# Bias loads issued from ScalarE behind the last probabilities, and the rows' factor ahead of SyncE's larger loads

## The chip, the cores and the metric

The kernel runs on one core of a Trainium2 chip. The metric is the device time of one execution in microseconds (us), lower is better; the figure of a kernel is the median of its runs. TensorE (PE) multiplies matrices, VectorE (DVE), ScalarE (ACT) and GpSimd (POOL) do elementwise work, and SyncE (SP) only issues DMAs here. ACT and POOL can issue DMAs as well. A profile says "SPq" or "ACTq" for work of an engine's sequencer, such as the issue of a DMA.

## What is computed

One block on 128 sequences of 128 tokens with 256 features, in float32: cross attention with 16 heads and a bias on the scores, and then a mixture of 8 experts of which each token uses one.

```python
x = x + tanh(g_xattn) * attn(layernorm(x), ctx, ctx, bias)   # bias: 128 x 16 x 128 x 128
x = x + tanh(g_ffn) * moe(layernorm(x))

# attn: q, k, v projections (low-rank parts added), D = 16
scores = einsum('bqhd,bkhd->bhqk', q * D ** -0.5, k) + bias
out = einsum('bhqk,bkhd->bqhd', softmax(scores), v)
# moe: idx = argmax(softmax(x @ Wg + bg)); out = (gelu(x @ W1[idx] + b1[idx])) @ W2[idx] + b2[idx]
```

The bias is by far the largest input: 128 x 16 x 128 x 128 numbers, which is 1 MB for each sequence.

## The kernel before

The attention goes through the sequences in order. Every engine has a `step(i, k)` of its own; step k of all engines together works on several sequences at different lags. `seq(i, k, lag)` is the sequence k - lag, so a negative lag means work ahead of time. There are 128 such steps and some more at either end; behind them comes the expert phase, from about 1700 us on. The queries and keys are projected for two sequences at a time, so steps come in pairs: even steps do more than odd ones.

**The rows' factor.** The layer norm of the queries is applied late: PE projects the raw x, and DVE multiplies the result by 1/sigma of each row (`scale_queries`, line 1104, which reads the tile `RS`). That factor is needed along the free dimension on all partitions, while it is computed one number to a partition. So it goes through device memory: for sequence k + 4, SP stores 128 numbers of 4 bytes each from `ln` (a part of `x2n`) to `rs_dram` (`send_scale`, line 357), waits until that store has landed (`rs_out`, line 365), and loads the row of 128 numbers back, broadcast to all partitions, into `RS` (`spread_scale`, line 367, 64 KB). The store waits for POOL's power (`rs_ok`, lines 507 and 509), which waits for DVE's statistics at the end of the step before.

**SyncE's queue.** All hardware-issued loads of the attention stand on SP's one queue, in the order of `step`: the factor's store, on even steps the context `CT` for two sequences (256 KB, line 380), `x_sb` (128 KB, line 385), on even steps `XT`, the turned x for the queries (256 KB, line 390), then the wait for the store and the load of `RS`, then the bias of sequence k + 3 into `sc` in two halves of 512 KB (line 403). The bias of k + 3 may be written once PE has turned all of sequence k - 1 (`tr_ready`), whose slot of four it takes.

**The other engines.** In step k DVE adds the bias to the scores (line 1039), takes the maxima (1045), then, once PE has turned the output (`o_ready`), the statistics of x of sequence k + 5 (1055, which needs `x_sb`), the residual (1152), on even steps `scale_queries` (1104), and the second statistics (1060, 1068). POOL subtracts the maxima (485), makes the norm factors (507, 509, 514), adds a bias to x (522), and scatters the rows of sequence k - 9 to `rows_dram` (540). A row buffer of eight is written again one step after its scatter is issued, so line 507 also waits for that scatter's landing (`x2_out`). ACT computes the probabilities of sequence k - 1 in four parts (`probs`, line 887), and each is behind PE's turning of that part.

Of the kernel before, what the change touches and what calls it, by code (L numbers as in the profile page):

```python
# [12 lines left out]
P = 128  # L13
# [3 lines left out]
HEADS = 16  # L17
# [6 lines left out]
U = 8  # L24
# [72 lines left out]
def flamingo_block(nc, x, x_turned, ctx_in, bias, wqT, wkT, wvT, bv, lora_in,  # L97
                   w1, w2, b2, consts, out):
    ctx = ExitStack()
    with ctx:  # L100
        def sb(name, shape, dt=F32):
            return ctx.enter_context(nc.sbuf_tensor(name, shape, dt))

        def sem(name):
            return ctx.enter_context(nc.semaphore(name))
# [29 lines left out]
        sc = sb("sc", [P, 4, HEADS * P])  # L135
# [107 lines left out]
        s_w, s_ab = {w: sem(f"s_w{w}") for w in "qkv"}, sem("s_ab")  # L243
# [7 lines left out]
        bias_in = [sem(f"bias_in{i}") for i in range(4)]  # L251
# [8 lines left out]
        tr_ready, pt_ready = sem("tr_ready"), sem("pt_ready")  # L260
# [35 lines left out]
        def seq(i, k, lag):  # L296

            t = At(i, k - lag, U)
            if isinstance(i, int) and not 0 <= i * U + k - lag < N:
                return None  # L300
            return t
# [45 lines left out]
        def _(sp):  # L347
# [6 lines left out]
            def send_scale(t):  # L354
                sp.wait_ge(rs_ok, t.n(1, 1))
                sp.nop(nofuse=True)
                sp.dma_start(rs_dram[t.n()], ln[:, (t.k - 7) % 8, 0, 0:1]).then_inc(rs_out, 16)  # L357
# [10 lines left out]

            def step(i, k):
                behind = seq(i, k, -4)  # L370
                if behind and not (isinstance(i, int) and k < 0):
                    send_scale(behind)
                t = seq(i, k, -6) if k > FIRST else None
                if t and t.slot(2) == 0:
                    if t.reached(8):
                        sp.wait_ge(k_ready, t.per(2, KC, -3 * KC))
                        sp.nop(nofuse=True)
                        sp.wait_ge(v_ready, t.n(1, -6))
                        sp.nop(nofuse=True)
                    sp.dma_start(CT[:, t.k // 2 % 4], ctx_in[t.per(2)]).then_inc(ctx_inn[t.k // 2 % 4], 16)  # L380
                if t:
                    if t.reached(8):
                        sp.wait_ge(x2_ok, t.n(1, -7))
                        sp.nop(nofuse=True)
                    sp.dma_start(x_sb[:, t.slot(8), :], x_seq[t.n()]).then_inc(x_in[t.slot(8)], 16)
                if behind and behind.slot(2) == 0:
                    if behind.reached(4):
                        sp.wait_ge(q_ready, behind.per(2, KC, -KC))
                        sp.nop(nofuse=True)
                    sp.dma_start(XT[:, behind.k // 2 % 2], x_turned[behind.per(2)]).then_inc(xT_in[behind.k // 2 % 2], 16)  # L390
                if behind and isinstance(i, int) and k < 0:
                    send_scale(behind)
                if behind:
                    spread_scale(behind)
                t = seq(i, k, -3)
                if t:
                    if t.reached(4):
                        sp.wait_ge(tr_ready, t.n(4, -12))  # L398
                        sp.nop(nofuse=True)
                    if not t.reached(1):  # L400
                        sp.wait_ge(s_w["k"], 16)
                    for h in range(0, HEADS, 8):
                        sp.dma_start(sc[:, t.slot(4), h * P:(h + 8) * P],  # L403
                                     bias[t.n(), :, h * P:(h + 8) * P]).then_inc(bias_in[t.slot(4)], 16)
                if isinstance(i, int) and k == 2:
                    sp.wait_ge(vacant_ok, 3)
                    sp.dma_start(rows_dram[DUMMY:DUMMY + FT, :].rearrange("(p a) r -> p (a r)", p=P),
                                 vacant[:]).then_inc(vacant_out, 16)
                    sp.dma_start(b2_all[:].rearrange("p e h -> p (e h)"), b2.rearrange("(a e) h -> a (e h)", a=1)
                                 .partition_broadcast(P)).then_inc(b2_in, 16)  # L410
# [428 lines left out]
        def _(act):  # L839
            for n in range(3):  # L840
                act.dma_start(lora[STRIP * n:STRIP * n + RANK, :], lora_in[n]).then_inc(s_ab, 16)
            for w, wt in (("v", wvT), ("q", wqT), ("k", wkT)):
                act.dma_start(W[w][:], wt).then_inc(s_w[w], 16)
            act.wait_ge(s_id, 16)
            nc.scalar.activation(tg[:], g_raw, ACT.Tanh).then_inc(s_seta, 1)

# [36 lines left out]
            def probs(t, q):  # L883
                act.wait_ge(tr_ready, t.n(4, q + 1))
                if q == 0 and t.reached(2):
                    act.wait_ge(ot_ready, t.n(1, -1))
                nc.scalar.activation(PT[:, t.slot(2), 512 * q:512 * q + 512], turn_bank(t, q)[:],  # L887
                                     ACT.Exp).then_inc(pt_ready, 1)

            def step(i, k):  # L890
# [42 lines left out]
                if prev and not scored:  # L933
                    probs(prev, 2)
                    probs(prev, 3)
                if qry and qry.slot(2) == 0:
                    queries(qry)

# [468 lines left out]
```

## Time and profile before

| what | us |
|---|---|
| median of 3 runs | 2010.56 (2008.79 to 2016.85) |
| the profiled execution | 2008.24 |
| its span | 2006.4 |
| PE, DVE, ACT, POOL busy | 1373.5, 1137.6, 774.8, 1000.9 |
| expert phase | from about 1700 to the end |

The span is what the profile covers; the execution's own time is 1.8 us more. Busy time is summed over both phases. A wait is listed as the engine and line that waited, and what ended the wait. The chain is followed back from the last instruction to whatever released each step. A landing time of a DMA runs from its issue to its completion. In a table of stretches, "DMA share" is the share of the 16 DMA engines' time that packets took.

### The profile page before, as it was taken

How to read it: one execution, taken by the hardware profiler on the slowest of the kernel's cores; microseconds unless marked ns; L12 is line 12 of the kernel's file. 1: busy time of each engine (PE TensorE's matmuls, PEld its weight loads, DVE VectorE, ACT ScalarE, POOL GpSimd, SP SyncE). 2: the span in 40 equal slices, each digit the busy share in tenths (PEclk: the TensorE clock that was granted, in tenths of full speed). 3: DMA queues.
4: the chain of work that ended last, by engine and by line, in shares of the span. 5: the costliest groups of instructions: out<-in, count | busy, mean ns of one | idle time of the engine just before them, and what ended most of it. 6: DMA issues, size and time to landing. Idle time of an engine off the chain costs nothing.

```text
span 2006.4 us, 41833 instructions
## 1 busy us (share of the span) xinstructions
PE 1373.5 (68%) x12568; PEld 1150.0 (57%) x12568; DVE 1137.6 (57%) x2377; ACT 774.8 (39%) x1660; POOL 1000.9 (50%) x1051
## 2 busy tenths in 40 slices
PE   4656666666666566666666656666666666999998
PEld 3545555555555455555555545555555555788887
DVE  3445555565655555556555555555555555855655
ACT  1333334444434334444443334444333344533333
POOL 2334544555554455455554544555445454655455
PEclk7777878888877778888887888888777788999999
DMA  4555655555555555556555555556555554599896
GB/s 114 125 120 126 132 129 119 115 130 130 131 131 114 122 129 128 102 129 131 131 128 110 128 128 123 110 126 131 121 114 131 129 129 113 198 297 278 277 284 212
DMA packets 156729, 288.73 MB, mean 144 GB/s; under 512 B 36836, under 2 KB 72166, under 8 KB 156544
## 3 DMA queue, kind: packets, MB, share of 16 engines
q1 hardware_dynamic: 142992, 252.02, 54.7%
q0 software_dynamic: 12624, 34.62, 4.7%
q10 hardware_dynamic: 1056, 1.39, 0.2%
q8 instruction: 28, 0.46, 0.1%
q14 instruction: 29, 0.24, 0.1%
HBM read 251.89 MB, written 36.98 MB: 144 GB/s over the span
## 4 chain that ended last, share of the span: by engine, by line
DMA 71%; PE 14%; SPq 9%; issue 5%; POOL 0%; DVE 0%; ACT 0%; POOLq 0%; ACTq 0%
DMA rs_dram<-x2n 70%; PE two L789 5%; PE bank L803 5%; SPq L403 5%; SPq L367 2%; PE two L777 1%; DMA RS<-rs_dram 1%; SPq L357 0%; PE two L596 0%; PE bank L630 0%; PE bank L621 0%; DMA w_sb<-in_w 0%; PE two L646 0%; SPq L398 0%; DMA rows_dram<-vacant 0%
## 5 line engine op out<-in xcount | busy, mean ns | idle before, releaser
L596 PE MATMUL two<-KT,QT 32*128 32x256 f32 x2048 | 206.1, 532 | 599.6 <-DVE QT L1104 564.0
L485 POOL TENSOR_TENSOR sc<-sc,negmax 128x1024 f32<-128x1024 f32 x256 | 484.1, 1893 | 149.9 <-DVE negmax L1045 144.3
L596 PEld LDWEIGHTS two<-KT,QT 32*128 32x128 f32 x2048 | 125.1, 250 | 636.6 <-DVE QT L1104 493.4
L1039 DVE TENSOR_TENSOR sc<-two,sc 128x1024 f32<-128x1024 f32 x256 | 312.1, 1219 | 130.2 <-PE two L596 128.8
L507 POOL TENSOR_SCALAR ve<-mv 128x2 f32<-128x2 f32 (+1 forms) x135 | 30.5, 226 | 667.8 <-DVE mv L1068 654.9
L1045 DVE TENSOR_REDUCE negmax<-sc 128x8 f32<-128x1024 f32 x256 | 312.4, 1220 | 16.2
L621 PE MATMUL bank<-cst,sc 128*128 128x128 f32 x2032 | 287.6, 287 | 0.1
L887 ACT ACTIVATE PT<-bank 128x512 f32<-128x512 f32 x508 | 279.5, 603 | 15.6 <-PE bank L621 14.4
L853 ACT ACTIVATE QT<-QT,cst 128x256 f32<-128x256 f32 x128 | 58.0, 500 | 559.4 <-DVE QT L1104 559.4
L621 PEld LDWEIGHTS bank<-cst,sc 128*128 128x128 f32 x2032 | 239.1, 148 | 32.7 <-issue 32.2
L1055 DVE BATCH_NORM_STATS2 st<-x_sb 128x6 f32<-128x256 f32 x128 | 53.9, 421 | 358.0 <-DMA x_sb<-in_x 356.1
L630 PE MATMUL bank<-PT,V 128*32 128x128 f32 x4096 | 181.9, 334 | 0.3 <-ACT PT L887 0.3
L555 POOL DMA_INDIRECT out<-og,ids x120 | 118.4, 986 | 115.0 <-issue 106.8
L1104 DVE TENSOR_TENSOR QT<-two,RS 128x256 f32<-128x256 f32 x128 | 48.3, 419 | 218.2 <-DMA RS<-rs_dram 218.2
L630 PEld LDWEIGHTS bank<-PT,V 128*32 128x32 f32 x4096 | 141.6, 137 | 48.6 <-issue 25.7
L881 ACT COPY OT<-bank 128x512 f32<-128x512 f32 x128 | 75.0, 586 | 231.0 <-PE bank L630 226.9
L540 POOL DMA_INDIRECT rows_dram<-x2n,slot_i x128 | 135.1, 1056 | 29.5 <-issue 25.4
L646 PE MATMUL two<-CT,wk 128*128 128x256 f32 x512 | 126.7, 391 | 13.0 <-DVE QT L1104 13.0
L864 ACT ACTIVATE KT<-two,bk_half,cst 128x256 f32<-128x256 f32 x256 | 124.0, 563 | 29.1 <-PE two L646 28.7
L746 PE MATMUL bank<-wv,CT 128*128 128x256 f32 x512 | 133.0, 383 | 0.0
L646 PE MATMUL two<-XT,wq 128*128 128x256 f32 x512 | 126.0, 389 | 4.4 <-DVE sc L1039 3.5
L803 PE MATMUL bank<-CT,hT 128*128 128x256 f32 x516 | 122.6, 379 | 0.0
(159 smaller groups left out, 2059.0 us busy)
## 6 DMA issues: line engine op xcount, KB each, us to landing
sc<-in_bias SPq DMA_DIRECT2D x256, 512.0 KB
w_sb<-in_w SPq DMA_DIRECT2D x69, 257.0 KB, 3.7
CT<-in_w SPq DMA_DIRECT2D x69, 256.0 KB, 3.8
xg<-rows_dram SPq DMA_DIRECT2D x63, 272.0 KB, 3.8
x_sb<-in_x SPq DMA_DIRECT2D x128, 128.0 KB, 11.0
CT<-in_ctx_in SPq DMA_DIRECT2D x64, 256.0 KB
XT<-in_x_turned SPq DMA_DIRECT2D x64, 256.0 KB
RS<-rs_dram SPq DMA_DIRECT2D x128, 64.0 KB
```

Source lines behind the costliest of these rows:

```text
L485: nc.gpsimd.tensor_tensor(s, s, m, ALU.add).then_inc(sub_ok, 1)
L540: nc.gpsimd.indirect_dma_start(rows_dram, bass.IndirectOffsetOnAxis(ap=slot_i[:, g, j:j + 1], axis=0), x2n[:, t.slot(8), :], None).then_in ...
L596: ins = mm(b_s[j][:, 2 * P * c:2 * P * c + 2 * P], QT[rows, pair, c, P * sq:P * sq + P], KT[rows, pair, c, sq].rearrange("p e k -> p (e k) ...
L621: ins = nc.tensor.transpose(turn_bank(t, q)[:, P * h:P * h + P], sc[:, t.slot(4), o:o + P], ident)
L630: ins = mm(b_x[CELL * j:CELL * j + CELL, P * (h // 4):P * (h // 4) + P], V[:, t.slot(8), h, :], PT[:, t.slot(2), P * h:P * h + P], start=T ...
L646: ins = mm(b_s[o][:, 0:2 * P], W[w][:, c, o * P:o * P + P], moving[:, c, :], start=(c == 0), stop=(c == KC - 1))
L746: ins = mm(b_v, CT[:, pair, c, tok:tok + P], W["v"][:, c, :], start=(c == 0), stop=(c == KC - 1))
L803: ins = mm(y_half, hT[:, t.slot(2), c, a * P:a * P + P], w2_of(t)[:, c * HID:c * HID + HID], start=(c == 0), stop=(c == KC - 1))
L864: ins = nc.scalar.activation(KT[:, pair, o, :, e, :], b_s[o][:, 0:2 * P].rearrange("p (s k) -> p s k", s=2), ACT.Identity, bias=bk_half[:, ...
L887: nc.scalar.activation(PT[:, t.slot(2), 512 * q:512 * q + 512], turn_bank(t, q)[:], ACT.Exp).then_inc(pt_ready, 1)
L1039: nc.vector.tensor_tensor(s, two[h][:], s, ALU.add).then_inc(s_used, 2)
L1045: nc.vector.tensor_reduce(negmax[:, t.slot(2), 8 * h:8 * h + 8], sc[:, t.slot(4), 1024 * h:1024 * h + 1024].rearrange("p (h k) -> p h k", ...
```

## The change

The bias loads leave SP. ACT issues them, for the first three sequences right after the weights, and from then on for sequence k + 3 at the end of ACT's step k, behind the last two probabilities of sequence k - 1 and ahead of the queries' bias. ACT has by then waited for PE's last turn of k - 1, so no wait is issued for it. On SP the load of `RS` moves up, right behind its store: it is now ahead of `CT`, `x_sb` and `XT` instead of behind them. For the very first steps the old place of the store holds one step less than before (k < -1 instead of k < 0).

```diff
@@ SP, step
-                if behind and not (isinstance(i, int) and k < 0):
+                if behind and not (isinstance(i, int) and k < -1):
                     send_scale(behind)
+                    spread_scale(behind)
...
-                if behind and isinstance(i, int) and k < 0:
+                if behind and isinstance(i, int) and k < -1:
                     send_scale(behind)
-                if behind:
                     spread_scale(behind)
-                t = seq(i, k, -3)
-                if t:
-                    if t.reached(4):
-                        sp.wait_ge(tr_ready, t.n(4, -12))
-                        sp.nop(nofuse=True)
-                    if not t.reached(1):
-                        sp.wait_ge(s_w["k"], 16)
-                    for h in range(0, HEADS, 8):
-                        sp.dma_start(sc[:, t.slot(4), h * P:(h + 8) * P],
-                                     bias[t.n(), :, h * P:(h + 8) * P]).then_inc(bias_in[t.slot(4)], 16)
@@ ACT, ahead of the steps
+            def load_bias(t):
+                for h in range(0, HEADS, 8):
+                    act.dma_start(sc[:, t.slot(4), h * P:(h + 8) * P],
+                                  bias[t.n(), :, h * P:(h + 8) * P]).then_inc(bias_in[t.slot(4)], 16)
+
+            for n in range(3):
+                load_bias(At(0, n, U))
@@ ACT, step
                 if prev and not scored:
                     probs(prev, 2)
                     probs(prev, 3)
+                t = seq(i, k, -3)
+                if t and t.reached(3):
+                    load_bias(t)
                 if qry and qry.slot(2) == 0:
                     queries(qry)
```

On SP, an odd step inside the loop, before. ISA and REGISTER_ALU rows are waits and address arithmetic; `sc<-in_bias` is the bias.

```order
L357 ISA [waits rs_ok]
L357 DMA rs_dram<-x2n 128x1
L385 ISA [waits x2_ok]
L385 DMA x_sb<-in_x 128x256
L364 REGISTER_ALU [waits scaled_ok]
L367 DMA RS<-rs_dram 128x128 [waits rs_out]
L398 REGISTER_ALU
L403 ISA [waits tr_ready]
L403 DMA sc<-in_bias 128x1024
L403 ISA
L403 DMA sc<-in_bias 128x1024
```

The same queue in the changed kernel, an even step and the start of the next.

```order
L357 ISA [waits rs_ok]
L357 DMA rs_dram<-x2n 128x1
L364 REGISTER_ALU [waits scaled_ok]
L367 DMA RS<-rs_dram 128x128 [waits rs_out]
L381 ISA [waits k_ready,v_ready]
L381 DMA CT<-in_ctx_in 128x512
L384 REGISTER_ALU
L386 ISA [waits x2_ok]
L386 DMA x_sb<-in_x 128x256
L391 DMA XT<-in_x_turned 128x512 [waits q_ready]
L357 ISA [waits rs_ok]
L357 DMA rs_dram<-x2n 128x1
```

Before, the bias stood between the load of `RS` and the next store; now the context, x and the turned x stand there, and the bias is gone from the queue.

On ACT, the end of an even step in the loop, before.

```order
L874 ACTIVATE x2n<-x,x2n 128x256 [waits x2t_ready,shift_ok]
L925 COPY V<-bank 128x16x16 [waits ot_ready,v_ready]
L931 COPY x2T<-two 128x256 [waits lt_ready,x2t_ready]
L887 ACTIVATE PT<-bank 128x512 [waits tr_ready] x2
L853 ACTIVATE QT<-QT,cst 128x256 [waits scaled_ok]
L853 ACTIVATE QT<-QT,cst 128x256
```

The same place in the changed kernel.

```order
L872 ACTIVATE x2n<-x,x2n 128x256 [waits x2t_ready,shift_ok]
L923 COPY V<-bank 128x16x16 [waits ot_ready,v_ready]
L929 COPY x2T<-two 128x256 [waits lt_ready,x2t_ready]
L885 ACTIVATE PT<-bank 128x512 [waits tr_ready] x2
L837 DMA sc<-in_bias 128x1024 x2
L851 ACTIVATE QT<-QT,cst 128x256 [waits scaled_ok]
L851 ACTIVATE QT<-QT,cst 128x256
```

Two DMA issues have come in behind the last two probabilities and ahead of the queries; nothing else moved on ACT. PE, DVE and POOL run the same instructions in the same order as before.

## Rows read from the trace of the kernel before

**Rows 1.** The page: busy time of the engines, and the chain by line.
```profile
PE 1373.5 (68%) x12568; PEld 1150.0 (57%) x12568; DVE 1137.6 (57%) x2377; ACT 774.8 (39%) x1660; POOL 1000.9 (50%) x1051
...
DMA rs_dram<-x2n 70%; PE two L789 5%; PE bank L803 5%; SPq L403 5%; SPq L367 2%; PE two L777 1%; DMA RS<-rs_dram 1%; SPq L357 0%; PE two L596 0%; PE bank L630 0%; PE bank L621 0%; DMA w_sb<-in_w 0%; PE two L646 0%; SPq L398 0%; DMA rows_dra
```
**Rows 2.** Who waited for whom: us in total, times, longest.
```profile
PE two L596 <- DVE QT L1104: 564.0, 61, 12.4
...
DVE st L1055 <- DMA x_sb<-in_x: 356.1, 102, 7.6
...
DVE QT L1104 <- DMA RS<-rs_dram: 218.2, 64, 10.0
...
SPq L365 <- DMA rs_dram<-x2n: 1166.8, 126, 11.9
```
**Rows 3.** The chain in order of time: start, us, what; two steps.
```profile
1006.43 0.33 SPq L367
...
1008.66 10.21 DMA rs_dram<-x2n
1019.01 0.33 SPq L367
...
1020.77 12.20 DMA rs_dram<-x2n
1033.11 0.33 SPq L367
```
**Rows 4.** The load of RS: durations of its issue, first and last start.
```profile
L367 SPq DMA_DIRECT2D RS<-rs_dram x128: 327/333/336, 16.0 to 1698.3; - x128
```
**Rows 5.** Busy time by stretch: PE, PEld, DVE, ACT, POOL, PE clock, DMA share, GB/s.
```profile
1020.00:1023.00 3.00, 3.00 (x57) 2.28 (x56) 2.30 (x6) 1.53 (x5) 1.94 (x3) 1.00 0.20 16
1023.00:1028.00 5.00, 4.87 (x33) 4.27 (x31) 3.82 (x5) 3.10 (x8) 4.76 (x5) 1.00 0.73 267
1028.00:1033.00 5.00, 0.00 (x0) 0.00 (x0) 0.00 (x0) 0.56 (x2) 1.00 (x1) 0.90 0.00 0
...
1012.00:1013.00 1.00, 1.00 (x12) 0.85 (x16) 0.80 (x6) 0.83 (x2) 0.22 (x1) 0.50 1.07 412
```
**Rows 6.** Instructions in order of time: start, us, what, idle time before it.
```profile
1009.35 0.78 SPq L380 DMA_DIRECT2D CT<-in_ctx_in  x1
...
1011.10 0.33 SPq L390 DMA_DIRECT2D XT<-in_x_turned  x1
1011.13 0.76 DVE L1104 TENSOR_TENSOR QT<-two,RS 128x256 f32<-128x256 f32 x2 [3.36 <-DMA RS<-rs_dram]
...
1019.68 0.86 SPq L403 DMA_DIRECT2D sc<-in_bias  x2
```
**Rows 7.** Chain and stretches at the start, before any bias was loaded.
```profile
15.98 0.33 SPq L367
...
16.88 8.28 DMA rs_dram<-x2n
...
20.00:25.00 5.00, 0.00 (x0) 0.00 (x0) 0.61 (x2) 0.00 (x0) 1.51 (x3) 0.67 0.00 0
...
9.00:10.00 1.00, 1.00 (x3) 0.82 (x4) 0.00 (x0) 0.00 (x0) 0.00 (x0) 0.50 0.96 350
```
**Rows 8.** DVE in order of time, from one step's start to the next stall.
```profile
1014.16 1.22 DVE L1039 TENSOR_TENSOR sc<-two,sc 128x1024 f32<-128x1024 f32 x1 [1.05 <-PE two L596]
...
1021.87 1.22 DVE L1039 TENSOR_TENSOR sc<-two,sc 128x1024 f32<-128x1024 f32 x1 [0.46 <-PE two L596]
...
1026.74 0.25 DVE L1141 RECIPROCAL rden<-bank 128x16 f32<-128x16 f32 x1
```
**Rows 9.** Landing times: x of 1000 to 1100 us, and the scatter issued at 1024.15.
```profile
DMA to landing us min/median/max: 10.3/10.8/11.2
...
1021.82 0.22 POOL L507 TENSOR_SCALAR ve<-mv 128x2 f32<-128x2 f32 x1 [0.82 <-DMA rows_dram<-x2n,slot_i]
...
1024.15 1.06 POOL L540 DMA_INDIRECT rows_dram<-x2n,slot_i  x1 [0.18 <-issue]
...
DMA to landing us min/median/max: 9.9/9.9/9.9
```

## The prediction, made before the changed kernel was run

> **What bounds the kernel now.** I read the chain by line first. The store of the rows' factor to device memory holds 70% of the span, while no engine is busy for more than 68% of it [rows 1]. The list of waits says the same: SyncE waited for that store 126 times, 1166.8 us in all. The long waits of the others hang on the same queue: DVE for x (356.1 us) and for the spread factor (218.2 us), and PE for the queries which DVE scales with that factor (564.0 us) [rows 2].
>
> The chain in order of time shows a loop inside one queue [rows 3]. The load of RS is issued at 1019.01, the next store at 1020.77, it lands at 1032.97, and the next load of RS is issued at 1033.11. The step before took 1006.43 to 1019.01. So a step is 12.6 and 14.1 us there. Over the whole phase there are 128 loads of RS from 16.0 to 1698.3 [rows 4]: 127 steps of 13.25 us. This is the period to change; the 308 us behind it are the expert phase, which the change does not touch.
>
> What fills the 14.1 us is seen in the stretches [rows 5]. From 1020 to 1023 the DMA engines move 16 GB/s: 3.0 us x 16 is 48 KB, nearly all of the 64 KB of RS. From 1023 to 1028 they move 267 GB/s, 1.3 MB: the bias, x and the scatter. From 1028 to 1033 they move nothing, and only then does the store land. Its data is 512 bytes. So the store has a tail of some 5.4 us of its own behind the last byte ahead of it, and the bias stands ahead of it because it was issued first on the same queue. The bias itself takes about 3.7 us: 1 MB at some 285 GB/s, between the 267 of that stretch and the 412 of the best microsecond.
>
> Is the tail the store's own, or a result of the bias? The start of the trace answers it [rows 7]. There only RS (issued 15.98) and one x load are ahead of the store issued at 16.88; no bias has been loaded yet. From 20 to 25 us the engines move nothing, and the store lands at 25.16. The tail is again over 5 us, with nothing around it. I conclude that the change can take the bias out of the path, and not the tail.
>
> **The change, part by part.** *The bias leaves SyncE's queue.* Its 3.7 us ahead of each store go, and the issue of two DMAs, 0.86 us [rows 6], which lay on the path too.
>
> *RS moves ahead, and CT, x and XT now stand between RS and the next store.* Before, they were behind the store and moved in its tail. Now they are ahead of it. For an odd step (RS, x, store) the trace has this very order at the start: from the issue of RS at 15.98 to the store's landing at 25.16 are 9.18 us [rows 7]. With 0.14 us from landing to the next issue of RS (1032.97 to 1033.11 [rows 3]) that is 9.3 us. An even step has CT and XT besides, 512 KB: at 412 GB/s [rows 5] 1.3 us, so 10.6 us. Their issue does not matter more: from CT at 1009.35 to the end of XT at 1011.43 are 2.1 us [rows 6], less than RS and its start-up take (4.7 us from its issue at 1006.43 to DVE's use at 1011.13 [rows 3, 6]). Mean of the two: 10.0 us.
>
> *The bias moves beside it, from another queue.* It still uses the same DMA engines. The cost lies between nothing (it moves in the store's 5.4 us tail, when the engines are idle) and its full 3.7 us (it moves while RS, x or CT are moving ahead of the store). Where does it fall? ACT issues it when PE has turned the last part, at the end of PE's step. PE starts a pair when RS has landed and DVE has scaled, about 5.6 us behind the issue of RS (RS issued at 1006.43, DVE's scaling from 1011.13 for 0.76 us [rows 3, 6]), and two steps of PE then take about 8 us each, as DVE's do [rows 8]. With steps of 10 us the two loads of a pair are thus issued some 3 to 5 us behind an issue of RS, and begin to move 1.6 us later (RS: issued 1006.43, bytes from about 1008). That is 5 to 10 us behind the issue of RS, mostly inside the tail, which by the rows above begins at 3.8 to 5.2 us. I take 0.5 us, near the lower end, as the rows of this phase put nearly all of it in the tail; an even step of before, with x, CT and XT moving in its tail, had a tail of about 5.9 instead of 5.4 us, which is the same 0.5. Both ends, 0 and 3.7, stay for the range. The period is then 10.5 us.
>
> *DVE, PE and POOL.* They run the same instructions. Undisturbed, DVE goes from one addition of the bias at 1014.16 to the next at 1021.87, 7.7 us, and reaches the reciprocal of the next step at 1026.74 [rows 8]; with the scaling of the queries and the scores behind it an even step is about 8.1. So 7.9 us a step is what the engines need, 2.6 us under the new period: they do not take over.
>
> *A second loop, through the scatter.* POOL's norm factors wait for the landing of a scatter that was issued a step earlier, 2.3 us behind the norm factors of that step (1021.82 and 1024.15 [rows 9]). The scatter of 1024.15 landed after 9.9 us at 1034.05, 1.1 us behind the store's landing at 1032.97 [rows 3, 9]; it seems to be held until the store is through. Suppose it still is: factors at 0, the next store 1.3 us later (0.22 and 0.72 us of work and some handing over, an estimate), 7.0 to 7.5 us for a store with an idle queue (start-up 1.6, tail 5.4), and 1.1 us to the scatter's landing: 9.4 to 9.9 us. That is just under 10.5, so it adds nothing, but it forbids much less than 9.4.
>
> *ACT* gets two issues a step, 0.86 us by SyncE's row; it is busy for 39% of the span [rows 1]. They stand ahead of the queries' bias, which is needed only a step later. If that cover were gone, it would cost up to 0.86 us on even steps, 55 us in all. The bias has three steps of slack, over 20 us, against a landing time like x's 10.8 [rows 9].
>
> *The start.* Three bias loads, 3 MB, now compete with the first inputs. At 350 GB/s [rows 7] they take 9 us, of which a part falls into the idle time under the first store's tail. I take 5 us, between 0 and 9. The step at k = -1 delays one x load by one store, which is inside this.
>
> The sum: 2008.2 (the profiled execution) - 127 x (13.25 - 10.5) + 5 = 2008.2 - 349.3 + 5 = 1664 us. The median of the runs is 2 us above that execution, so it comes to about 1665.
>
> **The rivals.** *Shorter than the sum (period 9.3).* CT and XT could move in the gaps which the slow broadcast of RS leaves (16 GB/s and a DMA share of 0.20 [rows 5]), and the bias wholly in the tail. Then each step is the 9.3 us of the start: 2008.2 - 127 x 3.95 + 5 = 1512 us. Against it stands the loop through the scatter, with 9.4.
>
> *Half of the bias collides (period 11.9).* The phase of ACT drifts so that half of the 3.7 us lies on RS, CT and x: 10.0 + 1.9 = 11.9, 2008.2 - 127 x 1.35 + 5 = 1842 us. For it: on odd steps the bias ends its move just where the next RS begins.
>
> *Only the issue time is saved (period 12.4).* The place in a queue might matter little, if all queues share the same engines and the store's packets wait behind the bias all the same. Then the 0.86 us of issue go and nothing else: 2008.2 - 127 x 0.86 + 5 = 1904 us. Against it stands that the store's landing follows the last byte of its own queue, and that the engines are idle for 5 of 14 us. The Trainium skill has such a rule, in "DMA: Bandwidth & Descriptors", section "Issuing engines are not separate DMA queues": DMAs issued from several engines run on the same 16 engines and interleave, and issuing from more of them saves sequencer time only. By that rule the time would be the one just given; the same page, section "Queues, rings and completion order", says that an engine takes turns between rings packet by packet, which would let a small store pass a large load. No run here shows yet which of the two holds for this store.
>
> *Slower (period about 14.1).* The bias moves in full while RS, x and CT are moving, and these have themselves come ahead of the store: 10.0 + 3.7, and 0.4 us more for the 139 KB of the scatter at some 350 GB/s, is 14.1 us: 2008.2 + 127 x 0.85 + 5 = 2121 us. It decides from the point where the bias delays the store by more than 13.25 - 10.0 = 3.25 us of its 3.7. The phase worked out above speaks against it.
>
> **How the numbers follow.** The sum with a period of 10.0 to 11.3: 0.55. Shorter: 0.15. Half: 0.14. Issue time only: 0.06. Slower or level: 0.10. The predicted time is 1665 us. The range from 1505 to 1850 holds the first three, 0.84, with their own edges a little cut. Two kernels of this kind can be told apart from about 0.5%, 10 us. All but the last case are faster by more: faster 0.90, same 0.02, slower 0.08.
>
> **What would show it.** The loads of RS should be 10.5 us apart, 9.3 to 10.0 on odd and 10.6 to 11.0 on even steps. The waits of SyncE for the store stay the longest, as does the store's part in the chain. A store's issue to landing should fall from 11 to about 8 us, and x's landing from 10.8 to under 6, since it is no longer behind a store. The engines' own waits for RS and x shrink from 13.25 - 7.9 = 5.3 to about 2.6 us a step. The bytes of the bias should be seen inside the store's tail. The forecast is wrong if the tail grows beside other traffic, if the bias is seen right behind an issue of RS, or if the wait for the scatter on line 507 becomes the longest: then the second loop decides.

## The result, and the profile after

| kernel | median us | runs |
|---|---|---|
| before | 2009.67 | 4 (2004.74 to 2016.85) |
| after | 1943.49 | 4 (1930.61 to 1947.13) |

The ratio is 0.9656, with a 95% interval from 0.9603 to 0.9710: faster by 3.4%, 66 us. 1665 us were forecast, and the time lies far above the range of 1505 to 1850. The sign is right; four fifths of the gain are missing.

The page of the changed kernel, the lines that answer to [rows 1], with the DMA queues between them (packets, MB, share of 16 engines):

```profile
PE 1444.8 (74%) x12568; PEld 1178.3 (61%) x12568; DVE 1157.2 (60%) x2377; ACT 785.1 (40%) x1660; POOL 998.7 (51%) x1051
...
q10 hardware_dynamic: 37920, 135.63, 50.7%
q1 hardware_dynamic: 106128, 117.78, 22.4%
...
DMA rows_dram<-x2n,slot_i 50%; DMA rs_dram<-x2n 13%; PE bank L793 5%; PE two L779 4%; POOL x2n L499 4%; DMA x_sb<-in_x 4%; DMA out<-og,ids 2%; POOL x_sb L512 2%; POOL ve L497 1%; PE two L767 1%; SPq L381 1%; SPq L386 1%; POOL x2n L504 0%; S
```

The bias is on its own queue now (q10). The store of the factor fell from 70% of the chain to 13%, and the scatter of the rows to device memory took its place with 50%. The waits (engine, line, what ended it: us in total, times, longest) against [rows 2]:

```profile
POOL ve L497 <- DMA rows_dram<-x2n,slot_i: 562.6, 106, 8.0
DVE st L1056 <- DMA x_sb<-in_x: 527.6, 116, 12.8
...
SPq L365 <- DMA rs_dram<-x2n: 1091.7, 115, 14.7
```

The same wait of POOL in the kernel before:

```profile
POOL ve L507 <- DMA rows_dram<-x2n,slot_i: 12.7, 14, 2.3
```

In [rows 2] SyncE waited 1166.8 us for its store in 126 waits, 9.3 us each; now it is 1091.7 in 115, 9.5 each. The wait has hardly moved. POOL's wait for the scatter was 12.7 us in all before; it is 562.6 now. DVE's wait for x was to shrink; it has grown, from 356.1 to 527.6 us. The load of RS, against [rows 4]:

```profile
L367 SPq DMA_DIRECT2D RS<-rs_dram x128: 327/333/358, 21.5 to 1630.8; - x128
```

127 steps in 1609.3 us are 12.67 us a step, where 13.25 stood and 10.5 was forecast. That is 0.58 x 127 = 74 us of gain less 5.5 us of a later start (21.5 against 16.0), 68 us, about the 66 that the spans differ by. The start cost what it was given.

One even step in order of time (start, us, what), from one load of RS to the next, with the issue of the bias by ScalarE:

```profile
1007.79 0.33 SPq L367 DMA_DIRECT2D RS<-rs_dram  x1
...
1009.12 0.33 SPq L386 DMA_DIRECT2D x_sb<-in_x  x1
...
1009.61 0.92 SPq L391 DMA_DIRECT2D XT<-in_x_turned  x1
...
1010.78 0.38 SPq L357 DMA_DIRECT2D rs_dram<-x2n  x1
1011.46 1.06 POOL L530 DMA_INDIRECT rows_dram<-x2n,slot_i  x1 [0.17 <-issue]
...
1014.45 0.84 ACTq L837 DMA_DIRECT2D sc<-in_bias  x2
...
1021.87 0.33 SPq L367 DMA_DIRECT2D RS<-rs_dram  x1
...
1022.71 0.22 POOL L497 TENSOR_SCALAR ve<-mv 128x2 f32<-128x2 f32 x1 [6.41 <-DMA rows_dram<-x2n,slot_i]
```

And what the DMA engines did from the bias's issue on (the last three columns are PE's clock, DMA share and GB/s):

```profile
1015.00:1022.00 7.00, 5.77 (x66) 4.47 (x58) 6.47 (x12) 1.69 (x4) 1.31 (x1) 1.00 0.96 29
1022.00:1026.00 4.00, 1.05 (x10) 1.05 (x10) 0.35 (x3) 1.38 (x4) 2.86 (x5) 1.00 0.77 257
```

The bias was issued at 1014.45, 3.7 us behind the store's issue, so that it should have moved in the store's tail, as the prediction had it. It did not. From 1015 to 1022 the engines moved 29 GB/s, which is 0.2 MB in seven microseconds, at a DMA share of 0.96: few packets moved, and these few took nearly all of the engines' time. When the store had landed, 1 MB went in four (257 GB/s). In [rows 5] the tail looked like idle time (0 GB/s, share 0.00). It was not free time: the load put there crawled until the store was through. Not every step is as clear: of the bias issued at 1002.44 about a third (at most 0.36 MB from 1004 to 1006, at 182 GB/s) moved while a store was in flight.

### The profile page after: what moved, and what is told of

Its sections match the earlier page's. It is cut to its first block, busy times and chain, and to the rows that moved or that the text cites. A ratio compares the mean times of both kernels' runs of the same rounds, so it can differ in the third digit from the quotient of the medians.

```text
span 1940.6 us, 41620 instructions
## 1 busy us (share of the span) xinstructions
PE 1444.8 (74%) x12568; PEld 1178.3 (61%) x12568; DVE 1157.2 (60%) x2377; ACT 785.1 (40%) x1660; POOL 998.7 (51%) x1051
## 3 DMA queue, kind: packets, MB, share of 16 engines
q10 hardware_dynamic: 37920, 135.63, 50.7%
## 4 chain that ended last, share of the span: by engine, by line
DMA 69%; PE 10%; POOL 8%; issue 7%; SPq 2%; DVE 1%; POOLq 1%; ACT 0%; DVEq 0%; ACTq 0%
DMA rows_dram<-x2n,slot_i 50%; DMA rs_dram<-x2n 13%; PE bank L793 5%; PE two L779 4%; POOL x2n L499 4%; DMA x_sb<-in_x 4%; DMA out<-og,ids 2%; POOL x_sb L512 2%; POOL ve L497 1%; PE two L767 1%; SPq L381 1%; SPq L386 1%; POOL x2n L504 0%; SPq L367 0%; DMA RS<-rs_dram 0%
## 5 line engine op out<-in xcount | busy, mean ns | idle before, releaser
L497 POOL TENSOR_SCALAR ve<-mv 128x2 f32<-128x2 f32 (+1 forms) x135 | 30.3, 225 | 718.2 <-DMA rows_dram<-x2n,slot_i 562.6
L1056 DVE BATCH_NORM_STATS2 st<-x_sb 128x6 f32<-128x256 f32 x128 | 54.1, 422 | 527.6 <-DMA x_sb<-in_x 527.6
L586 PE MATMUL two<-KT,QT 32*128 32x256 f32 x2048 | 199.5, 517 | 214.3 <-DVE QT L1105 154.0
L611 PE MATMUL bank<-cst,sc 128*128 128x128 f32 x2032 | 313.8, 305 | 1.5 <-issue 0.8
L611 PEld LDWEIGHTS bank<-cst,sc 128*128 128x128 f32 x2032 | 261.6, 158 | 35.2 <-issue 33.3
L872 ACT ACTIVATE x2n<-x,x2n 128x256 f32<-128x256 f32 x128 | 76.8, 600 | 388.2 <-POOL x2n L504 387.8
L636 PE MATMUL two<-XT,wq 128*128 128x256 f32 x512 | 144.9, 432 | 62.8 <-DVE sc L1040 32.7
L750 PE MATMUL two<-cst,x2n 128*128 128x128 f32 x256 | 58.8, 316 | 162.6 <-ACT x2n L872 159.6
L620 PEld LDWEIGHTS bank<-PT,V 128*32 128x32 f32 x4096 | 135.9, 133 | 49.1 <-issue 27.9
L636 PEld LDWEIGHTS two<-XT,wq 128*128 128x128 f32 x512 | 103.2, 212 | 86.0 <-issue 27.6
L750 PEld LDWEIGHTS two<-cst,x2n 128*128 128x128 f32 x256 | 32.7, 154 | 196.9 <-issue 165.7
L736 PE MATMUL bank<-wv,CT 128*128 128x256 f32 x512 | 139.7, 398 | 0.0
```

Of the source, the lines that this page charges most:

```text
L586: ins = mm(b_s[j][:, 2 * P * c:2 * P * c + 2 * P], QT[rows, pair, c, P * sq:P * sq + P], KT[rows, pair, c, sq].rearrange("p e k -> p (e k) ...
L611: ins = nc.tensor.transpose(turn_bank(t, q)[:, P * h:P * h + P], sc[:, t.slot(4), o:o + P], ident)
L620: ins = mm(b_x[CELL * j:CELL * j + CELL, P * (h // 4):P * (h // 4) + P], V[:, t.slot(8), h, :], PT[:, t.slot(2), P * h:P * h + P], start=T ...
L636: ins = mm(b_s[o][:, 0:2 * P], W[w][:, c, o * P:o * P + P], moving[:, c, :], start=(c == 0), stop=(c == KC - 1))
L736: ins = mm(b_v, CT[:, pair, c, tok:tok + P], W["v"][:, c, :], start=(c == 0), stop=(c == KC - 1))
```

## The experiments

The chips differ: the kernel before took 1951 to 2025 us on them. So whole times are compared by their ratio to before on the same chip, and within one chip where less than 2% matters. "Store to RS" is the time from the issue of a store to the issue of RS behind it, averaged over all steps from 300 to 1500 us of the trace; before has 11.47 us there and after 10.06, with steps of 13.30 and 12.75.

Four theories: **A**, the bias on its new queue delays the store. **B**, the scatter's landing is held behind the store, POOL's norm factors wait for it, and the next store waits for them. **D**, SyncE's wait for its own store sets the pace. **E**, what stands ahead of the store on its queue delays it. (The expectation of the first run also has a theory C: that is E at the prediction's price, 1.3 us on even steps and 0.4 on odd.) Expectations call the changed kernel "after". The kernels below that leave the bias or the store out, or store something else, are for timing alone.

### The two halves of the change

The bias moved, and RS where it was (the store issued, then CT, x, XT, then RS):

```diff
                     send_scale(behind)
-                    spread_scale(behind)
                 t = seq(i, k, -6) if k > FIRST else None
...
+                if behind:
+                    spread_scale(behind)
```

> The bias on ScalarE's queue as in the changed kernel, but the load of RS again behind CT, x and XT. Theory A (the bias still collides with the store, wherever RS stands): a period of about 12.7 us and 1940 us, as after. Theory B (the scatter's landing is held behind the store, and this loop sets the pace): also about 1940, since neither store nor scatter moves. Theory C (CT, x and XT ahead of the store cost what I reckoned, 1.3 us on even steps and 0.4 on odd): with them behind the store again the period falls by about 0.9 us, to 1830 us.

1796.71 us against 1955.63 for before: 0.9197 (0.9157 to 0.9237). Half the change is better than all of it. Since the chips differ, both were run again side by side.

> The changed kernel as the base on one chip for the next two. A ratio of 0.95 to 0.97.

> The bias on ScalarE's queue, the load of RS behind CT, x and XT as in the kernel before. If what stands ahead of the store on its queue delays it (theory E): 3 to 4% under the changed kernel on the same chip, a ratio of about 0.92 to before, and a store to RS 1.3 us shorter. If the earlier difference was the chips' (theory B or D alone): the same ratio as the changed kernel within 1%.

The changed kernel: 1879.16 us, 0.9614 (0.9558 to 0.9671). The bias alone: 1807.45 us, 0.9257 (0.9210 to 0.9303). The second half of the change costs 72 us, 3.8%, on one chip. Store to RS is 8.47 us with RS behind and 9.79 us with RS ahead: 1.3 us, as theory E has it. But the order changes a second thing: with RS ahead, SyncE stands and waits for its store before it issues x. DVE's wait for x, in the changed kernel and then with the bias alone, on this chip:

```profile
DVE st L1056 <- DMA x_sb<-in_x: 468.3, 114, 12.0
...
DVE st L1056 <- DMA x_sb<-in_x: 46.0, 27, 7.5
```

In the chain by line the load of x holds 4% of the changed kernel's span on this chip, 75 us, and is not among the pieces that the page of the other lists. So the late x is a rival to E for these 72 us, and no run separates the two.

The other half alone: RS ahead, and the bias on SyncE's queue at the end of the step.

```diff
-            for n in range(3):
-                load_bias(At(0, n, U))
...
-                t = seq(i, k, -3)
-                if t and t.reached(3):
-                    load_bias(t)
@@ SP, step
+                t = seq(i, k, -3)
+                if t:
...
+                    for h in range(0, HEADS, 8):
+                        sp.dma_start(sc[:, t.slot(4), h * P:(h + 8) * P],
+                                     bias[t.n(), :, h * P:(h + 8) * P]).then_inc(bias_in[t.slot(4)], 16)
```

> The load of RS ahead of CT, x and XT, the bias still on SyncE's queue at the end of the step. All of RS, CT, x, XT and bias are now ahead of the next store on one queue. By the terms of the prediction: 10.0 + 3.7 + 0.9 us of issue = 14.6 us a step, 2180 us. If the place of CT, x and XT costs nothing: 13.3 us, 2010 us.

2050.96 us, 1.0512 (1.0466 to 1.0557): slower than before. The sign follows from the queue's order. The size does not reach the 14.6 us a step of the terms, and lies between the two cases; the trace has 13.51 on a chip where before is 2.7% faster than in its profile.

### Is it the bias?

```diff
-                if t and t.reached(3):
+                if t and isinstance(i, int) and t.k == 3:
                     load_bias(t)
...
-                    dve.wait_ge(bias_in[t.slot(4)], t.per(4, 32, 32))
+                    dve.wait_ge(bias_in[t.slot(4)], 32)
+                    if t.reached(4):
+                        dve.wait_ge(tr_ready, t.n(4, -12))
```

> The changed kernel, but the bias is loaded for the first four sequences only; later ones add what is left in the tile. Theory A (the bias delays store, RS and scatter): the period falls to 10.0 or less, 1600 us. Theory B (store, then scatter, then the norm factors: a loop which the bias has no part in): the period stays at 12 or more, 1850 us or more.

1766.96 us against 1955.63 (one run): 0.904. Repeated beside the changed kernel on one chip:

> The changed kernel once more, as the base on the same chip for the three runs beside it. A ratio of 0.966 to before, and a store to RS of about 10 us.

> The changed kernel without the bias from the fifth sequence on, beside the changed kernel on one chip. If the bias delays the store (theory A): the time from store to RS is 1.5 to 2.5 us less than in the changed kernel, and the whole 150 to 200 us less. If the earlier difference was the chip's: both the same, within 0.5 us and 40 us. In both cases theory B or D keeps the step at 11 us or more without any bias.

The changed kernel: 1862.50 us, 0.9519 (0.9465 to 0.9574), store to RS 9.62 us. Without the bias: 1782.57 us, 0.9120 (0.9071 to 0.9169), store to RS 8.18. So the bias costs a store 1.4 us, and the whole 80 us, which is only 0.6 us a step: from RS to the next store it is 2.52 us with the bias and 3.39 without. But with no bias at all a step is still 11.57 us: theory A is a part, not the cause. In the kernel without the bias, one store and the scatter behind it (start, us, what):

```profile
1007.96 0.35 SPq L357 DMA_DIRECT2D rs_dram<-x2n  x1
1009.02 1.06 POOL L530 DMA_INDIRECT rows_dram<-x2n,slot_i  x1 [0.17 <-issue]
1016.08 0.33 SPq L367 DMA_DIRECT2D RS<-rs_dram  x1
...
1018.36 0.22 POOL L497 TENSOR_SCALAR ve<-mv 128x2 f32<-128x2 f32 x1 [4.49 <-DMA rows_dram<-x2n,slot_i]
1019.60 0.36 SPq L357 DMA_DIRECT2D rs_dram<-x2n  x1
```

and the DMA engines meanwhile:

```profile
1008.00:1011.00 3.00, 3.00 (x11) 2.53 (x11) 1.57 (x6) 1.19 (x4) 2.79 (x4) 0.59 0.69 241
1011.00:1016.00 5.00, 5.00 (x70) 4.10 (x69) 4.71 (x8) 3.53 (x9) 2.87 (x2) 1.00 0.00 1
```

The store takes 8.1 us with nothing moving from 1011 to 1016. The scatter's data is gone by 1011 too, yet POOL is released only at 1018.36, 2.3 us behind the store. Then 1.24 us to the next store. 8.1 + 2.3 + 1.2 = 11.6 us: this step is the second loop, term by term, and the mean step is 11.57. The Trainium skill, "DMA: Bandwidth & Descriptors", section "Queues, rings and completion order", states that a DMA's semaphore write lands only after every earlier write of that engine, across its queues. That the scatter, on another queue, lands only behind the store agrees with it.

Is the scatter slow by itself? Landing times of the scatters from 300 to 1000 us, as far as the profile records them: the kernel before, and then the kernel of the next section in which the store is left out.

```profile
DMA to landing us min/median/max: 5.6/9.3/10.9
...
DMA to landing us min/median/max: 2.9/3.6/5.0
```

It is not: without the store it takes 3.6 us.

The same with RS behind CT, x and XT:

> The same without the bias from the fifth sequence on. Theory E (order alone costs): as much under the changed kernel without the bias (0.91) as the kernel with the bias is under the changed one: 0.88. If the order costs only where the bias moves at the same time: 0.91, no better than without the bias in the changed order.

1860.59 us, 0.9541 (0.9484 to 0.9598). Neither case: without the bias this order is slower than with it (0.9257, same chip). Store to RS is 8.10 us, but RS to the next store has grown from 3.27 to 4.28. Its chain shows why it is slow, and not why that came about:

```profile
1008.57 10.07 DMA rows_dram<-x2n,slot_i
...
1021.27 8.64 DMA rows_dram<-x2n,slot_i
...
1032.49 10.55 DMA rows_dram<-x2n,slot_i
```

The whole step is the scatter, 8.6 to 10.6 us, and about 2.6 us of POOL and ScalarE's short part from its landing to the next issue. The first of the three landed 2.8 us behind the store (the next RS is issued at 1015.84, the scatter is through at 1018.64).

### Is it the store?

The store left out from the fifth sequence on:

```diff
-                sp.dma_start(rs_dram[t.n()], ln[:, (t.k - 7) % 8, 0, 0:1]).then_inc(rs_out, 16)
+                if not t.reached(4):
+                    sp.dma_start(rs_dram[t.n()], ln[:, (t.k - 7) % 8, 0, 0:1]).then_inc(rs_out, 16)
...
-                sp.wait_ge(rs_out, t.n(16, 16))
+                sp.wait_ge(rs_out, 64 if t.reached(4) else t.n(16, 16))
```

RS loads the first four rows again and again.

> The changed kernel, but the factor is stored for the first four sequences only; later ones load those four rows again. Theory A: RS no longer waits, but the bias still collides with x and the scatter: 10 to 11 us a step, 1650 us. Theory B: the scatter lands in 4 us as it does at the end of the phase, and the engines' own 8 us a step is reached: 1350 to 1400 us, with the bias in full flow.

1353.85 us (one run), 0.692 of before. The load of RS in this kernel:

```profile
L368 SPq DMA_DIRECT2D RS<-rs_dram x128: 319/331/332, 21.2 to 1037.1; - x128
```

8.0 us a step, the engines' own pace, with bias, x, CT, XT, RS and scatter all in flow. 512 bytes a step of stores, and the waits for them, account for all of the difference. The next two kernels keep the wait. Does it hang on the size of the pieces? Instead of 128 numbers of 4 bytes, 128 pieces of 512 bytes were stored, and in a second kernel 128 of 64 bytes (16 columns of the constants).

```diff
+        wide = nc.dram_tensor("wide", (P, P), F32, kind="Internal").ap()
...
+                if t.reached(4):
+                    sp.dma_start(wide, ident).then_inc(rs_out, 16)
...
```

They store a constant tile, always to the same place, and RS loads old rows as above.

> The changed kernel, but from the fifth sequence on the store writes 128 pieces of 512 bytes (a constant tile) to device memory instead of 128 pieces of 4 bytes, and RS loads old rows. If the 8 us come from the 4-byte pieces: the store lands in 3 to 4 us, near the 4.7 us of x's load, and the step falls to the engines' 8 us, 1360 to 1450 us. If they come from any write to device memory being waited for: 8 us or more as before, and the time stays at 1850 or more, the 64 KB adding to it.

> As the kernel with the wide store, but 128 pieces of 64 bytes. If any piece under 512 bytes is slow: a store to RS of 8 to 10 us and 1850 us or more. If only the 4-byte pieces are: near the wide store's 4.8 to 6.2 us and 1400 us.

1402.95 us with 512 bytes (0.693 of before), 1381.51 us with 64 (0.707 on another chip), one run each. Store to RS is 5.00 and 4.90 us. So it is neither the write to device memory nor any piece under 512 bytes: 128 times as many bytes land in half the 10.06 us of the changed kernel. Whether it is the 4 bytes as such, or that 128 such pieces lie side by side within 512 bytes of device memory, is not separated: size and place change together. With 64-byte pieces (start, us, what, and the stretches):

```profile
1012.53 0.84 ACTq L841 DMA_DIRECT2D sc<-in_bias  x2
...
1015.90 0.33 SPq L359 DMA_DIRECT2D wide<-cst  x1
...
1020.35 0.34 SPq L371 DMA_DIRECT2D RS<-rs_dram  x1
```
```profile
1016.00:1020.00 4.00, 4.00 (x32) 3.58 (x25) 3.93 (x4) 3.50 (x8) 3.80 (x4) 1.00 0.89 336
...
1019.00:1020.00 1.00, 1.00 (x6) 0.88 (x5) 1.00 (x1) 1.00 (x4) 1.00 (x1) 1.00 0.50 177
1020.00:1020.30 0.30, 0.30 (x4) 0.23 (x3) 0.30 (x3) 0.30 (x2) 0.12 (x2) 1.00 0.00 0
```

336 GB/s while this store is in flight, against 29 GB/s from 1015 to 1022 in the changed kernel, and the tail is gone: bytes move until 1020, and RS is issued at 1020.35. The two stretches are not quite alike, since here the bias was issued 3.4 us ahead of the store and there 3.7 us behind it. The whole traces say the same without that doubt. The queue of the bias in this kernel:

```profile
q10 hardware_dynamic: 37920, 135.63, 31.4%
```

The same packets and bytes as in the changed kernel took 31.4% of 16 engines over 1379.7 us, which is 433 us; there they took 50.7% of 1940.6, 984 us.

### The two loops around the store

POOL computes the queries' factor in a tile of its own, ahead of its wait for the scatter (cuts loop B):

```diff
                     if ahead:
                         pool.wait_ge(mv_ok[0], ahead.n(1, 1))
...
+                        nc.gpsimd.tensor_tensor(rsf[:, row:row + 1], ve[:, 0:1], minus_half[:], ALU.pow).then_inc(rs_ok, 1)
+                    if done:
+                        if done.reached(8):
+                            pool.wait_ge(x2_out[row], done.per(8, 16))
```

> The changed kernel, but POOL computes the queries' factor in a tile of its own, ahead of the wait for the scatter; the norm factors of the rows wait for it as before. Theory B (the loop from store to scatter to norm factors to the next store sets the pace): this loop is cut, and the queue's own loop is left: store 8.1 to 10 us and 1.7 to 2.4 us of issues behind it, 10.5 to 12 us a step; at least 0.7 us a step less than after, 1850 us or less. Theory D (SyncE's own wait for its store is the bound, the scatter only follows): no change from after, 12.7 us a step.

1940.16 us, 0.9599 (0.9559 to 0.9639): no different from the changed kernel's three ratios, 0.9519 to 0.9656. The 0.7 us a step were not there. Store to RS is 10.49 us and the step 12.59: as theory D has it, SyncE's own loop (10.49 and 2.10 us from RS to the next store) has nearly the same length, and the store holds 59% of the chain by line. With the bias in flow this loop alone keeps the step at 12.6 us.

SyncE issues RS one step behind its store, with a semaphore for even and one for odd sequences (cuts loop D):

```diff
                     send_scale(behind)
-                    spread_scale(behind)
+                sent = seq(i, k, -3)
+                if sent and (not isinstance(i, int) or k > -3):
+                    spread_scale(sent)
...
```

> The changed kernel, but SyncE issues the load of RS one step later than its store, so that it does not stand and wait for its own store. Theory D (that wait is the bound): the store leaves the path, 8 to 9 us a step, 1450 us or less. Theory B (the scatter's landing is held behind the store, and the next store waits for the norm factors behind it): 1.3 + 8.1 + 2.0 = 11.4 us a step as without the bias, or up to 12.5 with it: 1780 to 1930 us.

1870.64 us, 0.9257 (0.9219 to 0.9295), 12.23 us a step: theory B's case. SyncE's wait for the store is nearly gone, and it waits for POOL, which waits for the scatter, instead:

```profile
SPq L356 <- POOL x2n L502: 815.9, 124, 11.2
...
SPq L365 <- DMA rs_dram<-x2n: 42.4, 9, 13.3
```

Both at once:

> The changed kernel with both edits at once: the queries' factor apart from the norm factors that wait for the scatter, and the load of RS a step behind its store. If the two loops (SyncE's wait for its own store; store, scatter, norm factors, next store) are two bounds of nearly the same length, each hidden behind the other, cutting both frees more than either did alone: 10 us a step or less, 1600 us or less. If the store itself is the bound (one at a time, whoever waits): 11.5 to 12.2 us a step, 1800 to 1880 us.

1751.27 us, 0.8962 (0.8928 to 0.8996), 6.0% under the changed kernel on the same chip, and 11.29 us a step. More than either alone, yet neither of the two cases: short of the 10 us that two hidden bounds would free. SyncE's longest wait is now for DVE, which must be through with a tile of x before SyncE may load the next:

```profile
SPq L389 <- DVE x L1162: 807.3, 117, 12.0
```

The chain is shared out: the load of RS 22%, the scatter 16%, the store 9%. Which of these is the last bound was not taken further.

### Without any store

PE spreads the factor. The column of 128 numbers, broadcast, times the identity gives on every partition the row of 128 numbers; ScalarE copies it to RS.

```diff
+                    pe.wait_ge(rs_ok, qry.n(1, 2))
+                    for a in range(2):
+                        mm(b_s[0][:, 2 * P + P * a:3 * P + P * a],
+                           ln[:, (qry.k - 7 + a) % 8, 0, 0:1].broadcast_to([P, P]), ident, start=True, stop=True)
                     pe.wait_ge(xT_in[qry.k // 2 % 2], qry.per(4, 16, 16))
...
@@ ACT, ahead of the copy of the values
+                if qry and qry.slot(2) == 0:
+                    act.wait_ge(q_ready, qry.per(2, KC, 1))
+                    nc.scalar.copy(RS[:, qry.k // 2 % 2, :], b_s[0][:, 2 * P:4 * P]).then_inc(spread_in, 1)
```

On SP the calls of `send_scale` and `spread_scale` are gone, and DVE waits for `spread_in` before it scales.

> No store and no load of RS at all: two matmuls of the factor's column, broadcast, with the identity spread it over all partitions on PE, ahead of the projection of the queries, and ScalarE copies the result into RS. Bias on ScalarE's queue as in the changed kernel. Both theories: what e4_no_store has, 8 us a step and 1354 us, plus at most 0.6 us of PE a pair: 1350 to 1400 us. If the bias beside the other loads were a bound of its own it would stay over 1500.

1341.83 us, 0.6633 (0.6608 to 0.6659): 683 us under before on its chip, where the changed kernel has a ratio of 0.9519 to 0.9656. The page, and what the spreading costs from 300 to 900 us (busy us, mean ns of one):

```profile
PE 1269.7 (95%) x12824; PEld 1087.9 (81%) x12824; DVE 1116.2 (83%) x2377; ACT 795.1 (59%) x1724; POOL 1004.3 (75%) x1051
...
L716 PE MATMUL two<-cst,x2n 128*128 128x128 f32 x148 | 24.1, 285 | 0.0
...
L922 ACT COPY RS<-two 128x256 f32<-128x256 f32 x37 | 13.8, 373 | 25.5 <-PE two L633 25.5
```

The two matmuls of a pair stand in the trace as four instructions, 148 for 37 pairs: 24.1 us for 37 is 0.65 us of PE for two sequences, and 0.37 us of ScalarE.

## Why the prediction was wrong

**Right:** that the period of SyncE's queue is one bound, and that the start would cost about 5 us (5.5). x's landing fell from 10.8 to 4.7 us, as it was to. The bias was issued 4.5 and 6.7 us behind an issue of RS on the two steps looked at (3 to 5 were reckoned), in any case to fall into the tail.

The period was forecast at 10.5 us and measured 12.67. Two steps failed, and the second is the larger.

**Wrong, the first step: "the bias moves beside it, mostly inside the tail", at 0.5 us.** The tail of [rows 5] and [rows 7], 0 GB/s for 5 us, was read as idle engines. What it shows is engines on which nothing else was waiting. The load placed there went at 29 GB/s, and its megabyte was moved when the store was through. The bias costs a store 1.4 us (9.62 against 8.18 on one chip), where 0.5 were taken with 3.7 as the other end. In the period it is less: the changed kernel's loads of RS run from 22.8 to 1553.5 us on that chip, and without the bias from 21.2 to 1477.0, which is 12.05 and 11.46 us a step. So the 0.5 came near the 0.6 of the whole step, and that is luck: the reason given for it was wrong, and the store's growth is hidden in part by the other loop. The row that could have warned stood in the trace: in the stretches of before, from 1015 to 1020, the scatter of 139 KB and the rest of the loads moved at only 47 GB/s, beside a store that was issued at 1008.66 and landed at 1018.87:

```profile
1015.00:1020.00 5.00, 5.00 (x50) 4.45 (x42) 4.78 (x7) 4.25 (x10) 3.84 (x3) 1.00 0.35 47
```

**Wrong, the second step: "a second loop, through the scatter ... 9.4 to 9.9 us. That is just under 10.5, so it adds nothing."** Without any bias the prediction's period is 10.0; measured are 11.46 us, and this is the loop that makes it. The mechanism was right and became the longest piece of the chain, but two of its terms were too small. The store alone was put together as 1.6 + 5.4 = 7.0 to 7.5 us, though [rows 7] had it whole with 8.28; without the bias it measures 8.2. The lag of the scatter behind the store was taken from one row, 1.1 us. Over the 34 scatters of before, from 300 to 1500 us, whose landing the trace records, it is 0.3 to 2.9 us with 2.0 in the middle, and it measures 2.3 in the rows above. From RS to the next store it is 3.39 us without the bias, 1.2 from the norm factors on and so 2.1 for the lag: 1.2 + 8.2 + 2.1 is 11.5. With this loop cut and the bias in flow, SyncE's own loop still took 12.59 us, where 10.5 was forecast for it. So either of the two errors alone would have missed the period.

**A term that was near, and a question not asked: "even 10.6, odd 9.3"** for CT, x and XT ahead of the store. The sum had 0.7 us a step for it; on one chip it is 12.19 against 11.67 (loads of RS from 21.5 to 1569.7 and from 21.4 to 1503.1), 0.5 us. But it stayed a term: the prediction does not ask what the first half of the change does alone. It is the better kernel, by 3.8%, and the second half gives that back. The two means of store to RS differ by 1.3 us. That this is the whole reason is not shown, since x comes late too, and the same order without the bias is not faster.

**A loose reading:** 48 KB are three quarters of the 64 KB of RS, not nearly all. Nothing in the sum hangs on it.

**The rivals.** "Only the issue time is saved", with 1904 us and a chance of 0.06, comes nearest to the result. Its reason is not what was found: with RS where it was and the bias on its own queue, store to RS is 8.47 us where before has 11.47, though on another chip. So the bias did leave the path by more than its issue of 0.86. The Trainium skill states in "DMA: Bandwidth & Descriptors", section "Issuing engines are not separate DMA queues", that DMAs of different issuing engines run on the same 16 engines and interleave. These runs agree as far as that goes: the bias on ScalarE's queue and the store on SyncE's slow each other, 9.62 against 8.18 us for the store. What the forecast lacked was to turn the question round, and ask what the store does to the bias, and not only what the bias does to the store.

**Of the signs named:** the store's issue to landing was to fall from 11 to 8 us; it fell from 11.5 to 10.1. The waits of the engines for x and RS were to halve; the one for RS fell from 218.2 to 13.1 us, the one for x rose from 356.1 to 527.6, since x is now issued only when the store has landed. The wait on line 507 (now 497) for the scatter was named as the sign that the second loop decides: it is 562.6 us, the longest of the engines' waits.

**Left open:** why, without the bias, the scatter lags the store more when RS stands behind (RS to store 4.28 against 3.39 us), what holds 11.29 us when both loops are cut, how much of the second half's 0.5 us is the order on the queue and how much the late x, and whether the store is slow by the size of its pieces or by their lying side by side.

## What to carry to other kernels

When the longest wait is for a transfer of a few hundred bytes, change the transfer before you reorder what stands around it: here the store of 128 single numbers took 5 us more, beside the bias, than one of 128 pieces of 64 bytes, held the landing of the scatter on another queue, and 0.65 us of matmuls for two sequences did its work. A stretch in which DMA engines show no bytes is not free until a transfer put there has been seen to move. Of a change with two parts, price each alone; and when a second loop comes out within 10% of the forecast bound, take its terms from the whole rows that the trace has, since it will probably be the next bound.

## What was not expected of the hardware

- A store of 128 pieces of 4 bytes to device memory takes 8.2 us from issue to the next instruction, without the bias (5 of them with nothing moving at all, in the step shown), and 9.6 to 10.1 beside it; of 64 bytes it takes 4.9 us, of 512 bytes 5.0 us, these two beside the bias. The Trainium skill names 512 bytes, in "DMA: Bandwidth & Descriptors", section "Specifications", as the size below which a read-modify-write is made; in these runs 64 bytes were as fast as 512, and only the 4-byte pieces were slow. No run here shows whether a read-modify-write is the reason.
- Beside such stores the packets of another queue took 984 us of 16 engines' time for the 135.63 MB that took 433 us beside stores of 64-byte pieces; in one store's tail all queues together moved 29 GB/s.
- A scatter on GpSimd's queue whose bytes are through by 1011 released its waiter at 1018.36, 2.3 us behind the store. Without the store a scatter lands in 3.6 us.
- One and the same kernel differed between the chips of these runs by up to 3.8% (before: 1951 to 2025 us).
